# Rank 2 products of the gated layer's two projections, four at a time on the four row quarters of the array

## The chip, the cores and the metric

The kernel runs on one core of one Trainium2 chip. The metric is the device time of one execution in microseconds (us). The kernel before was timed three times.

## The reference

Four layers follow one another on a tensor x of 2 x 1024 tokens with 1024 channels, each as x = x + layernorm(layer(layernorm(x))). The change lies in the second of them, the gated layer. Cut to what matters:

```python
def _qlora_linear(x, wq, A, B):            # A: [2, in], B: [out, 2]
    w = jnp.tile(wq, (1, 4))               # wq: [out, in / 4]
    return x @ w.T + (x @ A.T @ B.T) * 0.5
gate = silu(_qlora_linear(x, w1q, a1, b1)) # w1q: [2752, 256]
up = _qlora_linear(x, w3q, a3, b3)
return _qlora_linear(gate * up, w2q, a2, b2)
```

Since the weight is tiled four times along the input, the kernel first adds the four parts of 256 input channels of x and multiplies the sum with the 256 columns of the quarter weight. The second term of each projection is a product of rank 2: two numbers a token (x @ A.T) times a row of B.

## The kernel before

The kernel is written in direct instructions with semaphores; each engine has one queue in a fixed order. The four layers are stages A, B, C and D. Stage B is the gated layer. It goes over 16 tiles of 128 tokens (t), and over 6 chunks (c) of 460 hidden columns (452 in the last). A pair (t, c) is a visit, numbered p = 6 t + c.

All large products are done in float32r. Each operand is split into a high part (rounded) and a low part (the rest), and three products are added: high x high, high x low, low x high. So a visit has, for the gate (v = 0) and for the up projection (v = 1), two halves of the 256 channels times three products, which are six matmuls of 128 rows, 128 tokens and 460 columns (lines 1126, 1127 and 1128 of `pe_up`).

To these comes one matmul for the rank 2 term (line 1133). Its stationary operand is `ux[:, par, v, :]`, 96 rows by 128 tokens; its moving operand is `bx[:, chunk]`, 96 rows by 460 columns. The rows of `bx` hold B of both projections three times, rounded in rows 0 to 31 and 64 to 95 and as the rest in rows 32 to 63 (`act_bhi` line 1211, `dve_blo` line 1339), and `ux` holds the two numbers a token rounded, rounded again, and the rest. With this the one matmul gives all three products. A visit of even number writes banks 0 (gate) and 1 (up) of PSUM, one of odd number banks 2 and 3. At its start a visit waits until the gate of visit p - 2 has read its banks (`gate_s(p - 1)`).

After a visit ScalarE takes the silu of the gate bank (`act_silu`, line 1259), VectorE multiplies it with the up bank (`dve_gate`, line 1356) and does two multiply and sum instructions for the rank 2 part of the third projection (`dve_acc`, line 1371), and GpSimd folds the product (`pool_gf`, lines 1469 and 1473).

Between the visits of tile t, TensorE also turns the folded result of tile t - 1 (`pe_gtr`, line 1146, after c = 0 and 2), multiplies it with the third weight (`pe_down`, lines 1159 to 1161, 18 matmuls of 512 columns after c = 3 and again after c = 4), and prepares tile t + 1:

- `pe_trans` (line 1088, after c = 1 and 2): transposes of x, which `act_xt` (line 1229) copies out.
- `pe_fold` (line 1099, after c = 3): x times A in float32, eight matmuls with 32 columns in the stationary operand, each four of them on the four column quarters of the array.
- `pe_low` (line 1107, after c = 4): two float32 matmuls with a constant matrix `sel`, which sum the four quarters, halve them and copy them to the rows where `ux` wants them, for v = 0 and v = 1. ScalarE reads the result with two instructions (`act_low`, lines 1250 and 1251), VectorE with one (`dve_low`, line 1350).

A float32 matmul is two records in the trace, a float32r matmul one.

The first tile of stage B (t = 0) stands between the last work of stage A. Its order is made by a planner (`plan`), which holds for each step an engine, a cost and the steps that it needs, and gives each engine a list. The planner orders the loads and stores of that time too: the load of `bx` (`sp_bx`), the stores of x (`stx`) and of its normalized form (`stn`), and the six loads of the third weight (`b_w2`). From t = 1 the order is the loops of `StageB.pe`, `act`, `dve` and `pool`. In tile 1 ScalarE also rounds the third weight (`act_w2hi`, line 1222) and VectorE and GpSimd form its rest (`w2lo`, line 1333).

Stage C is attention. Its matmuls with the values have 32 columns in the stationary operand and stand on the four column quarters as well (line 2001, float32). Its scores and maxima (lines 1986 and 1968) and its projections (lines 1944 to 1946) are float32r on the whole array.

Of the kernel before, what the change touches and what calls it, by code (L numbers as in the profile page):

```python
# [16 lines left out]
FH = 2752  # L17
# [236 lines left out]
class StageA:  # L254
# [78 lines left out]
    def plan(self):  # L333
# [102 lines left out]
        for c in range(3):  # L436
            add("act", .95, ("b_bhi", c), ("b_bx", 0), ("b_bhi", c - 1) if c else None)
            add("dve", 1.15, ("b_blo", c), ("b_bhi", c), ("b_blo", c - 1) if c else None)

        add("sp", 9.0, ("b_a2", 0), *(("conv", q, 2) for q in range(4)))  # L440
        add("sp", 3.5, ("b_bx", 0), ("down", 3, 3), ("center", 1, 8))
        add("sp", 1.0, ("b_a13", 0), layers, ("stn", 5))
# [5 lines left out]
        for t in range(2):  # L448
            for u in (2 * t, 2 * t + 1):
                add("pe", .5, ("b_tr", u), ("b_xn", t), ("b_xt", u - 1) if u % 2 else ("b_lowd", 0) if t else ("y", 12))  # L450
                add("act", .65, ("b_xt", u), ("b_tr", u), *((("b_fold", 0), ("b_xsum", 0)) if u == 2 else ()))
            add("pe", .9, ("b_fold", t), ("b_xt", 2 * t + 1), ("b_a13", 0))
            add("act", .3, ("b_usb", t), ("b_fold", t), ("b_low", 0) if t else None)
            add("pool", 2.1, ("b_xsum", t), ("b_xt", 2 * t + 1), ("b_xlo", 0) if t else None)
            add("act", .45, ("b_xhi", t), ("b_xsum", t))
            add("dve", .45, ("b_xlo", t), ("b_xhi", t))
            add("pe", .3, ("b_low", t), ("b_usb", t))
            add("act", .8, ("b_lowc", t), ("b_low", t))
# [524 lines left out]
class StageB:  # L983
# [3 lines left out]
    def __init__(self, k, first, x_src, xn_src, x_dst, xn_dst):  # L987
# [4 lines left out]
        with ExitStack() as ctx:  # L992
# [5 lines left out]
            self.w13l, self.w13h = sb("w13l", [128, 4 * FH], F32R), sb("w13h", [128, 4 * FH], F32R)  # L998
            self.bx = sb("bx", [96, FH], F32R)
            self.a13, self.sel = sb("a13", [128, 8, 32]), sb("sel", [128, 2, 96])  # L1000
            self.xnb = sb("xn", [128, 1024])
# [4 lines left out]
            self.usb = sb("usb", [128, 128])  # L1006
            self.ux, self.ur = sb("ux", [96, 2, 2, 128], F32R), sb("ur", [96, 2, 128], F32R)
            self.g = [sb(f"g{i}", [128, 460]) for i in range(3)]
            self.prod = [sb("pr0", [128, 460])]

            with nc.sbuf_tensor("b_bx_in", [96, FH], F32) as bx_in:
                self.bx_in = bx_in
# [30 lines left out]
    def sp_a13(self, e):  # L1043
        io = self.k.io
        e.dma_start(self.a13[:, :, :], io["a13T"].rearrange("(c p) n -> p c n", p=128)).then_inc(self.ldw.s, 16)
        e.dma_start(self.sel[:, :, :], io["sel"]).then_inc(self.ldw.s, 16)

# [55 lines left out]
    def pe_low(self, e, t):  # L1103
        e.wait_ge(*self.usb_s(t + 1))
        o = self.k.bank(5)
        for v in range(2):
            m = e.matmul(o[0:96, 128 * v:128 * v + 128], self.sel[:, v, :], self.usb[:, :], start=True, stop=True)
        m.then_inc(self.low_s.s, 1)

    def pe_up(self, e, t, c):  # L1110
# [3 lines left out]
        if t == 0:  # L1114
            e.wait_ge(*self.wlop_s(min(2 * c + 2, 6)))
            if c > 2:
                e.wait_ge(*self.wlod_s(2 * c - 4))
            if c < 2:
                e.wait_ge(*k.y_yn(self.first.tail.T + 14 + c))
        if p >= 2:  # L1120
            e.wait_ge(*self.gate_s(p - 1))
        wh, wl = self.chunk(self.w13h, c), self.chunk(self.w13l, c)
        for v in range(2):
            o = k.bank(2 * (p % 2) + v)[:, 0:n]
            for i in range(2):
                e.matmul(o, self.xsh[:, par, i, :], wh[:, v, i, :], start=i == 0, stop=False)  # L1126
                e.matmul(o, self.xsh[:, par, i, :], wl[:, v, i, :], start=False, stop=False)  # L1127
                e.matmul(o, self.xsl[:, par, i, :], wh[:, v, i, :], start=False, stop=False)  # L1128
# [73 lines left out]
    def act_bhi(self, e, i):  # L1202

        cols = slice(920 * i, min(920 * i + 920, FH))
        e.wait_ge(*self.ldb(1))
# [37 lines left out]
    def act_low(self, e, t):  # L1243
        e.wait_ge(*self.low_s(t + 1))
        if t > 0:
            e.wait_ge(*self.lowd_s(t))
        if t >= 2:
            e.wait_ge(*self.up_s(6 * (t - 1)))
# [87 lines left out]
    def dve_blo(self, e, i):  # L1336
        cols = slice(920 * i, min(920 * i + 920, FH))
        e.wait_ge(*self.bhi_s(i + 1))
        e.tensor_tensor(self.bx[32:64, cols], self.bx_in[32:64, cols], self.bx[32:64, cols].bitcast(F32), SUB
                        ).then_inc(self.blo_s.s, 1)  # L1340

# [5 lines left out]
    def dve_low(self, e, t):  # L1347
        e.wait_ge(*self.lowc_s(t + 1))
        o = self.k.bank(5)[:, 0:256].rearrange("p (v n) -> p v n", v=2)
        e.tensor_tensor(self.ux[64:96, t % 2, :, :], o[64:96], self.ur[64:96, :, :].bitcast(F32), SUB).then_inc(self.lowd_s.s, 1)  # L1350

# [1560 lines left out]
def lay_out(i):  # L2912
# [8 lines left out]
    cst[:, 256:384] = 1.0  # L2921
    cst[:, 384] = 1.0 / 128
    cst[:, 392:520] = np.where(np.arange(128)[None, :] > np.arange(128)[:, None], -1.0e38, 0.0)
    d["cst"] = cst
# [11 lines left out]
    d["w13"] = np.concatenate([w13[..., C0[c]:C0[c] + NS[c]].reshape(128, -1) for c in range(6)], 1)  # L2936
    bx = np.zeros((96, FH), f)
    for q in range(3):
        bx[32 * q:32 * q + 2] = g["L0_ffn_b1"][hid].T
        bx[32 * q + 2:32 * q + 4] = g["L0_ffn_b3"][hid].T  # L2940
    d["bx"] = bx
# [6 lines left out]
    d["w2x"] = np.concatenate([g["L0_ffn_w2q"].T, g["L0_ffn_b2"].T])  # L2948
    sel = np.zeros((128, 2, 96), f)
    for c in range(4):  # L2950
        for q in range(3):
            for r in range(2):
                sel[32 * c + r, 0, 32 * q + r] = 0.5
                sel[32 * c + 2 + r, 1, 32 * q + 2 + r] = 0.5
    d["sel"] = sel
# [26 lines left out]
```

## Time and profile before

| what | value |
|---|---|
| median of three runs | 2220.77 us (2220.75 to 2224.75) |
| the profiled execution, its own time | 2222.39 us |
| its span, first to last instruction | 2220.3 us |
| mean granted TensorE clock | 0.973 |
| busy: TensorE / its weight loads / VectorE / ScalarE / GpSimd | 93% / 67% / 64% / 43% / 45% |

A profile is of one execution. Busy time is the time in which an engine has at least one instruction under way. Matmuls are pipelined, so the record of one (about 0.37 us for 460 columns) overlaps the next; what a matmul costs in a dense stretch is the distance from its start to the next start. "PEld" is TensorE's weight load, which is a queue of its own beside the matmuls.

### The profile page before, as it was taken

Reading aid. Unit: us, or ns where it says so; the run is one execution under the profiler, and the core shown is the slowest. Engines: PE = TensorE matmul, PEld = TensorE weight load, DVE = VectorE, ACT = ScalarE, POOL = GpSimd, SP = SyncE. Lnnn points to the kernel's source line nnn. Section 1 sums busy time; section 2 is a strip of 40 time slices with the busy share of each in tenths; the row PEclk is TensorE's granted clock in tenths of the full one; section 3 lists DMA queues with packets and bytes.
Section 4 is the critical chain, followed back from the end, with each engine's and each line's share of the span. In section 5 each row is a group of like instructions: output and inputs, shape, how many; then the busy total and the mean of one; then the engine's idle time right before and its main releaser. Section 6 shows DMA issues by size and latency. Waiting matters only on the chain.

```text
span 2220.3 us, 30914 instructions
## 1 busy us (share of the span) xinstructions
PE 2057.5 (93%) x10568; PEld 1494.3 (67%) x10568; DVE 1411.5 (64%) x3276; ACT 955.2 (43%) x1990; POOL 997.1 (45%) x866
## 2 busy tenths in 40 slices
PE   5889987999999989989999999899998999999998
PEld 4645446788888879755556555555553688888887
DVE  6877766676776763387665677576768555544533
ACT  5755685232333323135554555455555332322311
POOL 1444586444444420018875586768873233120000
PEclk9999998999999999999999999999988999999999
DMA  6400275122211147422223723322223465544432
GB/s 186 172 2 29 101 248 213 39 76 77 74 67 68 68 173 272 121 53 55 68 71 100 212 66 78 78 77 72 52 68 121 137 225 174 167 161 138 134 117 92
DMA packets 148028, 249.78 MB, mean 112 GB/s; under 512 B 27150, under 2 KB 79246, under 8 KB 147648
## 3 DMA queue, kind: packets, MB, share of 16 engines
q1 hardware_dynamic: 136864, 227.89, 32.6%
q10 hardware_dynamic: 11008, 19.93, 2.9%
q8 instruction: 84, 1.38, 0.3%
q14 instruction: 72, 0.59, 0.1%
HBM read 140.01 MB, written 76.02 MB: 97 GB/s over the span
## 4 chain that ended last, share of the span: by engine, by line
PE 56%; POOL 15%; DVE 8%; issue 4%; DMA 3%; ACT 3%; SPq 1%; ACTq 1%; POOLq 0%; DVEq 0%
POOL c_S L2418 8%; PE PS L2609 4%; PE PS L2613 4%; PE PS L2610 4%; PE PS L1127 3%; PE PS L1126 3%; PE PS L1128 3%; PE PS L1986 3%; PE PS L1968 2%; PE PS L2001 2%; PE PS L1159 2%; PE PS L1161 2%; PE PS L1160 2%; DVE PS L2310 2%; PE PS L1944 2%
## 5 line engine op out<-in xcount | busy, mean ns | idle before, releaser
L2155 ACT ACTIVATE c_P<-PS 128x512 f32<-128x512 f32 (+3 forms) x768 | 357.3, 494 | 318.9 <-PE PS L1986 298.7
L1968 PE MATMUL PS<-c_K,c_Q 96*128 96x512 f32 (+3 forms) x768 | 276.2, 370 | 19.7 <-DVE cst L2310 13.9
L1986 PE MATMUL PS<-c_Q,c_K 97*128 97x512 f32 (+3 forms) x768 | 281.2, 380 | 7.0 <-DMA c_Q<-c_mT 4.3
L2418 POOL TENSOR_TENSOR c_S<-c_S,c_P 128x2048 f32<-128x2048 f32 (+3 forms) x94 | 272.7, 2901 | 8.6 <-ACT c_P L2155 0.2
L1986 PEld LDWEIGHTS PS<-c_Q,c_K 97*128 97x128 f32 x768 | 147.0, 194 | 174.4 <-ACT c_P L2155 97.2
L2306 DVE TENSOR_REDUCE cst<-PS 128x1 f32<-128x512 f32 x256 | 175.9, 687 | 91.4 <-PE PS L1968 91.0
L1968 PEld LDWEIGHTS PS<-c_K,c_Q 96*128 96x128 f32 x768 | 150.0, 196 | 75.0 <-DVE cst L2310 37.7
L2001 PE MATMUL PS<-c_P,c_V 128*32 128x512 f32 (+3 forms) x1536 | 168.2, 510 | 15.9 <-ACT c_P L2155 9.1
L2310 DVE CUSTOM_DVE_ANT_0 PS<-PS,maskw,cst 128x128 f32<-128x128 f32 (+3 forms) x256 | 142.8, 558 | 58.2 <-PE PS L1968 42.1
L213 POOL TENSOR_TENSOR maskw<-maskw,mhalf 128x1 f32<-128x1 f32 x64 | 38.6, 602 | 306.9 <-DVE maskw L171 297.9
L1259 ACT ACTIVATE b_g<-PS 128x460 f32<-128x460 f32 x96 | 53.0, 554 | 272.5 <-PE PS L1133 272.5
L2310 DVE CUSTOM_DVE_ANT_0 PS<-PS,maskw 128x128 f32<-128x128 f32 (+3 forms) x256 | 126.3, 503 | 63.0 <-PE PS L1968 61.2
L1371 DVE SCALAR_TENSOR_TENSOR b_pr<-b_g,b_a 128x460 f32<-128x460 f32 x192 | 159.9, 868 | 1.7
L2397 POOL TENSOR_SCALAR_AFFINE_SELECT c_P<-c_P 128x512 f32<-128x512 f32 x128 | 84.4, 660 | 159.2 <-ACT c_P L2155 159.2
L1469 POOL TENSOR_TENSOR b_gp<-b_g 128x230 f32<-128x230 f32 x96 | 84.5, 880 | 157.0 <-DVE b_g L1356 157.0
L1126 PE MATMUL PS<-b_w13h,b_xsh 128*128 128x460 f32 (+1 forms) x384 | 148.4, 386 | 5.4 <-ACT a_yl L230 3.3
L2609 PE MATMUL PS<-c_xth,d_xh 128*128 128x512 f32 x384 | 151.3, 394 | 0.0
L2610 PE MATMUL PS<-c_xtl,d_xh 128*128 128x512 f32 x384 | 150.1, 391 | 0.0
L1127 PE MATMUL PS<-b_w13l,b_xsh 128*128 128x460 f32 (+1 forms) x384 | 144.1, 375 | 0.0
L1128 PE MATMUL PS<-b_w13h,b_xsl 128*128 128x460 f32 (+1 forms) x384 | 143.2, 373 | 0.0
L1944 PE MATMUL PS<-c_xth,c_wh 128*128 128x512 f32 x304 | 125.5, 413 | 4.9 <-POOL c_wl L2239 2.3
L1356 DVE TENSOR_TENSOR b_g<-b_g,PS 128x460 f32<-128x460 f32 x96 | 60.4, 629 | 97.6 <-ACT b_g L1259 97.5
(301 smaller groups left out, 4887.8 us busy)
## 6 DMA issues: line engine op xcount, KB each, us to landing
a_xin<-in_x SPq DMA_DIRECT2D x32, 512.0 KB, 4.6
d_x<-scr SPq DMA_DIRECT2D x32, 512.0 KB, 4.8
c_Q<-c_qh SPq DMA_DIRECT2D x240, 64.0 KB, 2.0
scr<-a_xin SPq DMA_DIRECT2D x16, 512.0 KB, 6.7
b_xn<-scr SPq DMA_DIRECT2D x16, 512.0 KB, 5.7
b_x<-scr SPq DMA_DIRECT2D x16, 512.0 KB, 4.8
scr<-b_x SPq DMA_DIRECT2D x16, 512.0 KB, 2.6
scr<-b_y SPq DMA_DIRECT2D x16, 512.0 KB, 3.0
```

Source lines behind the costliest of these rows:

```text
L1126: e.matmul(o, self.xsh[:, par, i, :], wh[:, v, i, :], start=i == 0, stop=False)
L1127: e.matmul(o, self.xsh[:, par, i, :], wl[:, v, i, :], start=False, stop=False)
L1128: e.matmul(o, self.xsl[:, par, i, :], wh[:, v, i, :], start=False, stop=False)
L1968: e.matmul(bank[:, 0:hi - lo], self.Q4[0:96, 4 * (o % 3) + g, 128 * t:128 * t + 128], self.K4[0:96, HEADS[o % 8], lo:hi], start=True, stop ...
L1986: e.matmul(self.k.bank(i % 3)[:, 0:hi - lo], self.K4[0:97, HEADS[o % 8], 128 * kt:128 * kt + 128], self.Q4[0:97, 4 * (o % 3) + g, lo:hi], ...
L2001: m = e.matmul(k.bank(5)[32 * g:32 * g + 32, lo - 512 * half:512], self.V[:, kt, o // 8, HEADS[o % 8], :], P[:, g, 0:hi - lo], start=kt == ...
L2155: e.activation(self.P[:, R % 3, g, 0:hi - lo], self.k.bank(i % 3)[:, 0:hi - lo], ACT.Exp, scale=SCALE).then_inc(self.exp_s.s, 1)
L2306: e.tensor_reduce(m, r, AX, ALU.max).then_inc(self.mx_s.s, 1)
L2310: e.tensor_tensor_reduce(out=r, in0=r, in1=self.maskw[:, 512 - n:512], scale=1.0, scalar=m if lo > 0 else -3.0e38, op0=ADD, op1=ALU.max, a ...
L2418: e.tensor_tensor(S[:, :, 512 - n:512], S[:, :, 512 - n:512], P[:, :, 0:n], ADD).then_inc(self.psum_s.s, 1)
L2609: e.matmul(o, h, wh[:, c, cols], start=c == 0, stop=False)
L2610: e.matmul(o, h, wl[:, c, cols], start=False, stop=False)
```

## The change

The three products of a rank 2 term need only six rows of the array, so they fit in one quarter of 32 rows. The kernel after puts the gate and the up projection of an even chunk in row quarters 0 and 1, and those of the odd chunk behind it in quarters 2 and 3. Four matmuls with 32 rows each (`tile_position=(32 * s, 0)`) write banks 0, 1, 2 and 3. They are issued one after another at the end of the even visit, as the last addends of banks 0 and 1 and the first addends of banks 2 and 3; the odd visit has no rank 2 matmul. Before the four, TensorE waits for `gate_s(p)`, the gate of the odd visit before, since banks 2 and 3 are written now; the odd visit has no wait of its own any more. In tile 0 the wait for stage A's last users of banks 2 and 3 moves from visit 1 to the four in visit 0.

`ux`, `ur`, `bx` and `sel` change their form: `ux` is 128 rows by 128 tokens a tile (before: 96 rows by 256), `bx` is 128 rows by 3 x 460 columns (before: 96 by 2752), `sel` one matrix of 128 by 128 (before: two of 128 by 96), so `pe_low` is one float32 matmul, `act_low` one copy of 128 by 128, and `dve_low` and `dve_blo` one scalar_tensor_tensor over all 128 rows with a mask as scalar. Three unused tensors keep the later addresses about where they were. The planner's costs and conditions follow.

```diff
-                ("b_up", c - 1) if c else None, ("b_gate", c - 2) if c > 1 else ("y", 13 + c))
+                ("b_up", c - 1) if c else None, ("b_gate", c - 1 - c % 2) if c > 1 else ("y", 14))
...
     def pe_low(self, e, t):
         e.wait_ge(*self.usb_s(t + 1))
         o = self.k.bank(5)
-        for v in range(2):
-            m = e.matmul(o[0:96, 128 * v:128 * v + 128], self.sel[:, v, :], self.usb[:, :], start=True, stop=True)
-        m.then_inc(self.low_s.s, 1)
+        e.matmul(o[:, 0:128], self.sel[:, :], self.usb[:, :], start=True, stop=True).then_inc(self.low_s.s, 1)
...
-            if c < 2:
-                e.wait_ge(*k.y_yn(self.first.tail.T + 14 + c))
-        if p >= 2:
+            if c == 0:
+                e.wait_ge(*k.y_yn(self.first.tail.T + 14))
+        if p >= 2 and c % 2 == 0:
             e.wait_ge(*self.gate_s(p - 1))
         wh, wl = self.chunk(self.w13h, c), self.chunk(self.w13l, c)
+        late = c % 2
         for v in range(2):
-            o = k.bank(2 * (p % 2) + v)[:, 0:n]
+            o = k.bank(2 * late + v)[:, 0:n]
             for i in range(2):
...
-            if c == 0 and v == 0:
-                e.wait_ge(*self.lowd_s(t + 1))
-            if t == 0 and c % 2 == 0 and v == 0:
-                e.wait_ge(*self.blo_s(c // 2 + 1))
-            m = e.matmul(o, self.ux[:, par, v, :], self.bx[:, C0[c]:C0[c] + n], start=False, stop=True)
-        m.then_inc(self.up_s.s, 1)
...
+        if late:
+            m.then_inc(self.up_s.s, 1)
+        else:
+            self.pe_rank(e, t, c // 2)
+
+    def pe_rank(self, e, t, j):
+
+        k, p, par = self.k, 6 * t + 2 * j, t % 2
+        if j == 0:
+            e.wait_ge(*self.lowd_s(t + 1))
+        if t == 0:
+            e.wait_ge(*self.blo_s(j + 1))
+            if j == 0:
+                e.wait_ge(*k.y_yn(self.first.tail.T + 15))
+        if p > 0:
+            e.wait_ge(*self.gate_s(p))
+        for s in range(4):
+            n, rows = NS[2 * j + s // 2], slice(32 * s, 32 * s + 32)
+            m = e.matmul(k.bank(s)[:, 0:n], self.ux[rows, par, :], self.bx[rows, 460 * j:460 * j + n], start=s > 1, stop=s < 2,
+                         skip_group_check=True, tile_position=(32 * s, 0))
+            if s == 1:
+                m.then_inc(self.up_s.s, 1)
...
-        o = self.k.bank(5)[:, 0:256].rearrange("p (v n) -> p v n", v=2)
-        e.copy(self.ux[0:64, t % 2, :, :], o[0:64])
-        e.copy(self.ur[64:96, :, :], o[64:96]).then_inc(self.lowc_s.s, 1)
+        e.copy(self.ur[:, :], self.k.bank(5)[:, 0:128]).then_inc(self.lowc_s.s, 1)
...
-        e.tensor_tensor(self.ux[64:96, t % 2, :, :], o[64:96], self.ur[64:96, :, :].bitcast(F32), SUB).then_inc(self.lowd_s.s, 1)
+        if t >= 2:
+            e.wait_ge(*self.up_s(6 * (t - 1)))
+        e.scalar_tensor_tensor(out=self.ux[:, t % 2, :], in0=self.k.bank(5)[:, 0:128], scalar=self.k.cst[:, 385:386],
+                               in1=self.ur[:, :].bitcast(F32), op0=MUL, op1=SUB).then_inc(self.lowd_s.s, 1)
```

## Rows read from the trace of the kernel before

**Rows 1.** Windows by stage: length, busy (instructions) by engine, clock, DMA share, GB/s

```profile
380.00:420.00 40.00, 32.77 (x150) 28.11 (x151) 26.65 (x47) 12.57 (x22) 22.34 (x21) 0.83 0.09 27
750.00:780.00 30.00, 30.00 (x164) 26.13 (x163) 21.68 (x49) 8.78 (x16) 13.09 (x17) 1.00 0.25 85
```

**Rows 2.** Waits, 450 to 800 us: total us, times, longest

```profile
ACT b_g L1259 <- PE PS L1133: 212.8, 73, 5.4
```

**Rows 3.** The critical chain in order of time: start, us, what

```profile
329.06 0.86 PE PS L617 x2
...
393.87 0.76 PE PS L1159
...
489.03 0.44 PE PS L1107 x4
...
773.96 0.44 PE PS L1107 x4
...
793.99 0.23 PE PS L1160
...
807.76 0.56 ACT b_g L1259
```

**Rows 4.** TensorE, timeline 602 to 613 us: start, duration, line

```profile
602.84 0.60 PE L1107 MATMUL PS<-b_usb,b_sel 128*96 128x128 f32 x4
603.20 0.48 PE L1159 MATMUL PS<-b_w2h,b_gfh 115*128 115x512 f32 x1
603.52 0.40 PE L1160 MATMUL PS<-b_w2l,b_gfh 115*128 115x512 f32 x1
...
610.27 0.37 PE L1126 MATMUL PS<-b_w13h,b_xsh 128*128 128x460 f32 x1
...
612.99 0.38 PE L1133 MATMUL PS<-b_bx,b_ux 96*128 96x460 f32 x1
```

**Rows 5.** TensorE, timeline around the fold on four column quarters

```profile
623.30 0.37 PE L1133 MATMUL PS<-b_bx,b_ux 96*128 96x460 f32 x1
623.60 0.64 PE L1099 MATMUL PS<-b_xT,b_a 128*32 128x128 f32 x16
624.17 0.50 PE L1159 MATMUL PS<-b_w2h,b_gfh 115*128 115x512 f32 x1
624.51 0.39 PE L1160 MATMUL PS<-b_w2l,b_gfh 115*128 115x512 f32 x1
```

**Rows 6.** TensorE, timeline around a group of stage C on column quarters

```profile
1301.43 0.28 PE L1968 MATMUL PS<-c_K,c_Q 96*128 96x256 f32 x1
1301.65 1.06 PE L2001 MATMUL PS<-c_P,c_V 128*32 128x512 f32 x8
1302.64 0.44 PE L1986 MATMUL PS<-c_Q,c_K 97*128 97x384 f32 x1
1302.92 0.34 PE L1968 MATMUL PS<-c_K,c_Q 96*128 96x384 f32 x1
```

**Rows 7.** The weight loads of that group, timeline

```profile
1301.64 0.16 PEld L2001 LDWEIGHTS PS<-c_P,c_V 128*32 128x32 f32 x8 [0.20 <-issue]
1302.64 0.19 PEld L1986 LDWEIGHTS PS<-c_Q,c_K 97*128 97x128 f32 x1 [0.84 <-ACT c_P L2155]
```

**Rows 8.** Weight loads by line: ns min/median/max, first and last start

```profile
L1133 PEld LDWEIGHTS PS<-b_bx,b_ux x192: 187/188/334, 340.8 to 807.2; 96*128 96x128 f32 x192
...
L2001 PEld LDWEIGHTS PS<-c_P,c_V x1536: 106/109/155, 981.4 to 1736.4; 128*32 128x32 f32 x192
```

**Rows 9.** VectorE, timeline: the gate of a tile's last visit

```profile
611.05 0.62 DVE L1356 TENSOR_TENSOR b_g<-b_g,PS 128x452 f32<-128x452 f32 x1 [1.75 <-ACT b_g L1259]
```

**Rows 10.** Tiles 0 and 1: TensorE, ScalarE and GpSimd rows

```profile
348.00 0.72 PE L1126 MATMUL PS<-b_w13h,b_xsh 128*128 128x460 f32 x1 [3.29 <-ACT a_yl L230]
...
378.43 1.99 ACT L1222 CAST b_w2h<-b_w 115x1024 fp32r<-115x1024 f32 x2 [6.87 <-DMA b_w<-in_w2x]
...
L1333 POOL TENSOR_TENSOR b_w2l<-b_w,b_w2h x3: 2356/3322/3354, 379.6 to 390.5; 115x1024 fp32r<-115x1024 f32 x3
```

More of the change, by code:

```diff
@@ L436, in plan @@
         for c in range(3):
-            add("act", .95, ("b_bhi", c), ("b_bx", 0), ("b_bhi", c - 1) if c else None)
-            add("dve", 1.15, ("b_blo", c), ("b_bhi", c), ("b_blo", c - 1) if c else None)
+            add("act", .5, ("b_bhi", c), ("b_bx", 0), ("b_bhi", c - 1) if c else None)
+            add("dve", .65, ("b_blo", c), ("b_bhi", c), ("b_blo", c - 1) if c else None)
         add("sp", 9.0, ("b_a2", 0), *(("conv", q, 2) for q in range(4)))
-        add("sp", 3.5, ("b_bx", 0), ("down", 3, 3), ("center", 1, 8))
+        add("sp", 2.5, ("b_bx", 0), ("down", 3, 3), ("center", 1, 8))
         add("sp", 1.0, ("b_a13", 0), layers, ("stn", 5))
@@ L457, in plan @@
             add("pe", .3, ("b_low", t), ("b_usb", t))
-            add("act", .8, ("b_lowc", t), ("b_low", t))
+            add("act", .3, ("b_lowc", t), ("b_low", t))
             add("dve", .45, ("b_lowd", t), ("b_lowc", t))
@@ L998, in __init__ @@
             self.w13l, self.w13h = sb("w13l", [128, 4 * FH], F32R), sb("w13h", [128, 4 * FH], F32R)
-            self.bx = sb("bx", [96, FH], F32R)
-            self.a13, self.sel = sb("a13", [128, 8, 32]), sb("sel", [128, 2, 96])
+            self.bx = sb("bx", [128, 3 * 460], F32R)
+            sb("gap0", [128, 1368])
+            self.a13, self.sel = sb("a13", [128, 8, 32]), sb("sel", [128, 128])
+            sb("gap1", [128, 64])
             self.xnb = sb("xn", [128, 1024])
@@ L1006, in __init__ @@
             self.usb = sb("usb", [128, 128])
-            self.ux, self.ur = sb("ux", [96, 2, 2, 128], F32R), sb("ur", [96, 2, 128], F32R)
+            self.ux, self.ur = sb("ux", [128, 2, 128], F32R), sb("ur", [128, 128], F32R)
+            sb("gap2", [128, 384])
             self.g = [sb(f"g{i}", [128, 460]) for i in range(3)]
             self.prod = [sb("pr0", [128, 460])]
-            with nc.sbuf_tensor("b_bx_in", [96, FH], F32) as bx_in:
+            with nc.sbuf_tensor("b_bx_in", [128, 3 * 460], F32) as bx_in:
                 self.bx_in = bx_in
@@ L1045, in sp_a13 @@
         e.dma_start(self.a13[:, :, :], io["a13T"].rearrange("(c p) n -> p c n", p=128)).then_inc(self.ldw.s, 16)
-        e.dma_start(self.sel[:, :, :], io["sel"]).then_inc(self.ldw.s, 16)
+        e.dma_start(self.sel[:, :], io["sel"]).then_inc(self.ldw.s, 16)
     def sp_a2(self, e):
@@ L1125, in pe_up @@
             for i in range(2):
-                e.matmul(o, self.xsh[:, par, i, :], wh[:, v, i, :], start=i == 0, stop=False)
-                e.matmul(o, self.xsh[:, par, i, :], wl[:, v, i, :], start=False, stop=False)
-                e.matmul(o, self.xsl[:, par, i, :], wh[:, v, i, :], start=False, stop=False)
-            if c == 0 and v == 0:
-                e.wait_ge(*self.lowd_s(t + 1))
-            if t == 0 and c % 2 == 0 and v == 0:
-                e.wait_ge(*self.blo_s(c // 2 + 1))
@@ L1133, in pe_up @@
-            m = e.matmul(o, self.ux[:, par, v, :], self.bx[:, C0[c]:C0[c] + n], start=False, stop=True)
-        m.then_inc(self.up_s.s, 1)
+                e.matmul(o, self.xsh[:, par, i, :], wh[:, v, i, :], start=i == 0 and not late, stop=False, skip_group_check=True)
+                e.matmul(o, self.xsh[:, par, i, :], wl[:, v, i, :], start=False, stop=False, skip_group_check=True)
+                m = e.matmul(o, self.xsl[:, par, i, :], wh[:, v, i, :], start=False, stop=i == 1 and bool(late),
+                             skip_group_check=True)
@@ L1202, in act_bhi @@
     def act_bhi(self, e, i):
-        cols = slice(920 * i, min(920 * i + 920, FH))
+        cols = slice(460 * i, 460 * i + 460)
         e.wait_ge(*self.ldb(1))
@@ L1336, in dve_blo @@
     def dve_blo(self, e, i):
-        cols = slice(920 * i, min(920 * i + 920, FH))
+        cols = slice(460 * i, 460 * i + 460)
         e.wait_ge(*self.bhi_s(i + 1))
-        e.tensor_tensor(self.bx[32:64, cols], self.bx_in[32:64, cols], self.bx[32:64, cols].bitcast(F32), SUB
-                        ).then_inc(self.blo_s.s, 1)
+        e.scalar_tensor_tensor(out=self.bx[:, cols], in0=self.bx_in[:, cols], scalar=self.k.cst[:, 386:387],
+                               in1=self.bx[:, cols].bitcast(F32), op0=MUL, op1=SUB).then_inc(self.blo_s.s, 1)
     def dve_xlo(self, e, t):
@@ L2922, in lay_out @@
     cst[:, 384] = 1.0 / 128
+    for s in range(4):
+        cst[32 * s + 4:32 * s + 6, 385] = 1.0
+        cst[32 * s + 2:32 * s + 4, 386] = 1.0
     cst[:, 392:520] = np.where(np.arange(128)[None, :] > np.arange(128)[:, None], -1.0e38, 0.0)
@@ L2936, in lay_out @@
     d["w13"] = np.concatenate([w13[..., C0[c]:C0[c] + NS[c]].reshape(128, -1) for c in range(6)], 1)
[L2937 to L2940, printed above, removed]
+    bx = np.zeros((128, 3 * 460), f)
+    for c in range(6):
+        rows, cols = 64 * (c % 2), 460 * (c // 2)
+        for q in range(3):
+            for v, n in enumerate(("L0_ffn_b1", "L0_ffn_b3")):
+                bx[rows + 32 * v + 2 * q:rows + 32 * v + 2 * q + 2, cols:cols + NS[c]] = g[n][hid[C0[c]:C0[c] + NS[c]]].T
     d["bx"] = bx
@@ L2948, in lay_out @@
     d["w2x"] = np.concatenate([g["L0_ffn_w2q"].T, g["L0_ffn_b2"].T])
-    sel = np.zeros((128, 2, 96), f)
+    sel = np.zeros((128, 128), f)
     for c in range(4):
[L2951 to L2954, printed above, removed]
+        for s in range(4):
+            for q in range(3):
+                for r in range(2):
+                    sel[32 * c + 2 * (s % 2) + r, 32 * s + 2 * q + r] = -0.5 if q else 0.5
     d["sel"] = sel
```

3 lines of the change are left out of this document (removed).

## The prediction

> **What bounds the kernel now.** I read the windows by stage first. From about 394 to 808 us TensorE is busy all the time at the full clock of 2.4 GHz, while VectorE is busy 22 of 30 us, and DMA a quarter of the time; in 380 to 420 us TensorE has gaps and a granted clock of 0.83 [rows 1]. The waits say the same: ScalarE waits 213 of 350 us for the rank 2 matmul that ends a visit [rows 2]. The chain of waits is TensorE alone, and gives the period: `pe_low` of one tile starts at 489.03, that of the tenth after it at 773.96, so a tile takes 28.49 us [rows 3]. Whatever a tile loses on TensorE in this stretch shortens the kernel, until another engine is late.
>
> Two ends have to be drawn. At the start, tile 0 and most of tile 1 are not TensorE's: ScalarE waits 6.9 us for the third weight's load until 378.43, GpSimd's last part of its rest starts at 390.5 and takes 3.3 us [rows 10], and the first `pe_down` of stage B starts at 393.87 [rows 3]. What TensorE saves before 393.87 is waited away. The stage's last silu is at 807.76 [rows 3], and what follows (the last tile's way out, stage C's first tiles) starts from it, so I take the saving as passed on in full. Between lie, of the changed pieces: the four of visit 4 of tile 1, three groups of four in each of tiles 2 to 15, so 43 groups, and `pe_low` in tiles 1 to 14, 14 times.
>
> **What is removed: four rank 2 matmuls in a row of visits.** From visit 0's first start at 610.27 to its 14th at 612.99 are 13 steps, 0.209 us each [rows 4]. The record's 0.37 us is not the cost, since records overlap. Four cost 0.837 us.
>
> **What is added: one group on row quarters.** No group on row quarters stands in this trace. The nearest are groups on column quarters, in two places. In stage C, four float32 matmuls of 512 columns [rows 6]. Before it, the 256 column matmul steps 0.22 us where by columns (0.23 us for 512 in the chain, L1160 at 793.99) it should be 0.12 [rows 3]: 0.10 to enter. The group takes 0.99; one float32 matmul of 512 columns alone takes 0.86 in the chain [rows 3], so the four do run side by side, with 0.13 over one. Behind it the 384 column matmul steps 0.28 instead of 0.17: 0.11 to leave. Sum over the stream: 0.34. The fold gives the same: 0.30 instead of 0.21 on entering, 0.57 for two float32 matmuls of 128 columns in series (2 x 0.86 / 4 = 0.43), 0.34 instead of 0.23 on leaving, again 0.34 [rows 5]. What the entry and exit are is seen in the weight loads: in a dense stretch a load starts a matmul ahead, but the group's first load starts only at 1301.64, with the matmul, after a pause of 0.20, and the load behind it at 1302.64, with its matmul too [rows 7]. So neither is hidden.
>
> The changed group streams 460 columns once: 0.209. To this the 0.34, and its first load is longer: 188 ns for 128 columns against 109 for 32 [rows 8], so 0.08. The group costs 0.63, and saves 0.837 - 0.63 = 0.21 us; times 43 is 9.0 us. The eight loads of the group in stage C lie within 0.16 us, 0.05 more than one, so 7 ns apart [rows 7]; I take it that loads on row quarters overlap so too.
>
> Bounds. Below: nothing for entering and leaving, 0.209 + 3 x 0.007 = 0.23, saves 0.61 a group, 26 us. Above, in two steps. Loads that follow one another: (188 - 109) / 96 columns is 0.82 ns a column [rows 8], 0.105 for 128, three times 0.32, so the group is 0.95 and loses 0.11, 5 us in all. And matmuls that don't run side by side at all: 0.837 + 0.34 + 0.08 = 1.26, loses 0.42, 18 us. I take the value between since it is the one that both places of the trace give, with the same 0.34.
>
> The Trainium skill, page "TensorEngine Tiling (Array Packing)", Key Properties, says that a change of the tiling mode, not of the tile alone, drains TensorE. The trace agrees for column quarters, by the 0.10 on entering and on leaving. By this rule the sum stays at 9.0 us; it speaks against the small groups of this change, of which each pays both ways.
>
> **`pe_low`: two float32 matmuls to one.** Four records start at 602.84, the next line's first at 603.20 and second at 603.52 [rows 4]; less one step of 0.23 for the latter the four cost 0.45. Half of it goes: 0.22 x 14 = 3.1 us. The load is of 128 columns instead of 96; half of 0.45 for two passes leaves 0.11 a load, just enough for 0.105. Bounds 1.5 and 3.1 us.
>
> **Other edits.** `act_low` (one instruction instead of two), `dve_low` and the casts of `bx` lie beside a TensorE that is the later one, and don't set the end; ScalarE waits over half of the time [rows 2]. If that cover were gone they would gain less than 1 us a tile, not lose. The matmuls' count and columns in the visits stay. `dve_low` now holds the wait for `up_s` of the tile before, which is long passed.
>
> **Waits that move.** The group waits for the gate of the odd visit before it. Behind it in the queue stands all of TensorE. The tightest is visit 0: its twelve other matmuls end 12 x 0.209 = 2.5 us after 610.27, at 612.78, and the gate of the last visit ends at 611.05 + 0.62 = 611.67 [rows 4, 9]. Slack 1.1 us. After the other odd visits stand transposes or a `pe_down`, so more. In tile 0 the group waits for stage A's y, for which visit 1 waited 3.29 us until 348.00 [rows 10]; so visit 0 ends and its silu starts some 5.6 us later than before. Cover: ScalarE's 6.9 us for the third weight [rows 10]. That load's place in SP's queue comes from the planner, behind stores of stage A that a late VectorE or GpSimd moves; with fewer and shorter steps, but later ones, I take zero, and 3 us on either side for the range.
>
> **Sum.** Span 2220.3 - 9.0 - 3.1 = 2208.2. The profiled execution took 2222.39, 1.6 above the median of 2220.77, so its time would be 2210.3 and the median 2208.7 us.
>
> **Rivals.**
> 1. Loads hidden, no entry or exit: the group's four loads start under the full matmul before, as loads in a dense stretch do, and the next full load starts under the group. For it: with whole-array matmuls the trace shows just this. Against it: at both places with quarters it doesn't [rows 5, 7]. 26 + 3.1 us less: 2191.5 us. The page "TensorE: Matmul & The Clock Gate" of the Trainium skill, Part 3, The mechanism, has the loads pulled ahead where row groups don't conflict, and starts some 4 ns apart; its measured speedup of four row quarters (3.07) would make 0.27 of the 0.837, so 24 us; no run here shows it yet.
> 2. Half of it: only entering or leaving is paid. 0.43 a group, saves 0.41, 17.5 us and 3.1: 2200 us.
> 3. The other side: the row quarters' loads or matmuls stand in line. The change decides against itself when a group costs over 0.837 + 3.1 / 43 = 0.91 us. With loads in line 0.95: 5 - 3.1 = 2 us more, 2222.7. With matmuls in line: 18 - 3.1, 2235.7. For it: no row shows row quarters at work; against it, the column quarters' loads lie 7 ns apart.
> 4. A new wait: the gate of visit 5 comes later than the group. Each 0.1 us beyond the slack of 1.1 costs 15 x 0.1 = 1.5 us; from 0.9 us beyond it the gain of 12 is gone. For it: VectorE is busy 72% [rows 1] and the tile gets 4% shorter. Against: the slack is as long as the gate and the silu together.
> 5. The gain is real but lost on the way to the end, at the load of the third weight or at stage C's first loads: 2217 to 2223.
>
> **Chances.** Forecast (2204 to 2213 by itself) 0.42; rival 1 0.20; rival 2 0.12; rival 3 0.12, a third of it with matmuls in line; rival 4 0.06; rival 5 0.08. A measurement of this kernel tells 0.2%, 4.4 us, from no change. Faster by more than that: 0.42 + 0.20 + 0.12 and a little of 4: 0.75. Within: two thirds of rival 3, most of 5, some of 4: 0.14. Slower: 0.11. The range goes from rival 1 to loads in line: 2190 to 2222; only matmuls in line and the worst of 4 and 5 are outside, and some of the faster side.
>
> **What the profile after would show.** Right: a tile's period, `pe_low` to `pe_low`, of 28.49 - 3 x 0.21 - 0.22 = 27.64 us; the first of the four some 0.31 behind the last full matmul's start; the four starts within 0.03 us, their loads too; the matmul behind the group 0.1 late. A period of 26.4 is rival 1, 28.6 rival 3 with loads in line. Rival 4 would show as idle TensorE before the group in visit 0, released by VectorE's gate. The first `pe_down` should stay within 3 us of 393.87. Wrong would be the prediction above all by the group's cost: each 0.1 us of it is 4.3 us of time.

## The result, and the profile after

The kernel after takes 2203.61 us (median of six runs, 2199.94 to 2205.72), the kernel before, run beside it, 2221.57 us. The ratio is 0.9914 with a 95% interval of 0.9900 to 0.9927, so about 18 to 19 us are gained. The forecast was 2208.7 us, that is 12.1 gained.

The profiled execution after took 2203.54 us, its span is 2201.4 us, 18.9 less than before. The windows by stage (length, busy time of TensorE, its loads, VectorE, ScalarE, GpSimd, granted clock, DMA share, GB/s) answer to [rows 1]:

```profile
380.00:420.00 40.00, 36.48 (x190) 29.58 (x189) 27.10 (x53) 10.32 (x19) 22.94 (x23) 0.87 0.07 27
750.00:780.00 30.00, 30.00 (x147) 24.89 (x147) 22.39 (x54) 7.09 (x12) 13.18 (x18) 1.00 0.14 53
```

TensorE still has no gap in the stage and the full clock, but its loads are busy 24.9 of 30 us instead of 26.1. The chain of waits from tile 0 on, and its end in stage B (start, us, what), answers to [rows 3]:

```profile
355.10 17.69 DMA b_w<-in_w2x
...
388.27 0.77 PE PS L1178
...
788.86 0.56 ACT b_g L1274
```

The same row of the kernel before:

```profile
361.48 16.93 DMA b_w<-in_w2x
```

The third weight's last load is issued at 355.10 (361.48 before) and takes 17.7 us. The first down product is at 388.27 instead of 393.87, the last silu at 788.86 instead of 807.76. From the one to the other are 400.6 us instead of 413.9, 13.3 less; behind the last silu stand 2201.4 - 788.9 = 1412.5 us, and 2220.3 - 807.8 = 1412.5 before, so in these two executions what the stage gains reaches the end in full. The other 5.6 us are gained before the first down product. The loads of x's tiles in stage A, with SP's stores between them left out (timeline of SP), show how they split:

```profile
252.09 0.38 SPq L141 DMA_DIRECT2D a_xin<-in_x  x1
...
346.96 0.33 SPq L141 DMA_DIRECT2D a_xin<-in_x  x1
```

```profile
250.73 0.38 SPq L141 DMA_DIRECT2D a_xin<-in_x  x1
...
342.02 0.33 SPq L141 DMA_DIRECT2D a_xin<-in_x  x1
```

The first fence is the kernel before, the second the kernel after. The load of tile 4 is 1.4 us earlier already, far from any change; that of tile 15 4.9 us earlier. From the load of tile 4 to the first down product are 141.8 us before and 137.5 after: 4.2 us are gained there, and 1.4 come from how this execution began: in the fourteen executions below that load is issued between 250.6 and 255.2.

The group itself, TensorE's timeline behind the last matmuls of visit 0 and of visit 2:

```profile
599.92 0.36 PE L1130 MATMUL PS<-b_w13h,b_xsl 128*128 128x460 f32 x1
600.22 0.48 PE L1150 MATMUL PS<-b_bx,b_ux 32*128 32x460 f32 x4
600.63 0.69 PE L1165 MATMUL PS<-cst,b_gf 128*115 128x128 f32 x4
...
606.41 0.37 PE L1130 MATMUL PS<-b_w13h,b_xsl 128*128 128x460 f32 x1
606.71 0.48 PE L1150 MATMUL PS<-b_bx,b_ux 32*128 32x460 f32 x4
607.12 0.47 PE L1165 MATMUL PS<-cst,b_gf 128*115 128x128 f32 x2
607.43 0.60 PE L1091 MATMUL PS<-cst,b_xn 128*128 128x128 f32 x4
```

The kernel before, behind the rank 2 matmul of visit 2:

```profile
619.71 0.37 PE L1133 MATMUL PS<-b_bx,b_ux 96*128 96x460 f32 x1
619.92 0.38 PE L1146 MATMUL PS<-cst,b_gf 128*115 128x128 f32 x2
620.14 0.60 PE L1088 MATMUL PS<-cst,b_xn 128*128 128x128 f32 x4
```

The first of the four starts 0.30 us behind the matmul before, not 0.21: 0.09 to enter. All four lie in 0.48 us, where one record alone has 0.47 (below), so they start within 0.01 us. The next line starts 0.41 later, and its two records take 0.31 (607.12 to 607.43) where the same two took 0.22 in the kernel before (619.92 to 620.14). That is 0.09 + 0.41 + 0.09 = 0.59 us a group. The loads of the two groups (timeline of the weight loads), and by line over the whole kernel (ns min/median/max):

```profile
600.22 0.19 PEld L1150 LDWEIGHTS PS<-b_bx,b_ux 32*128 32x128 f32 x4 [0.31 <-issue]
600.63 0.49 PEld L1165 LDWEIGHTS PS<-cst,b_gf 128*115 128x115 f32 x4 [0.22 <-issue]
...
606.70 0.19 PEld L1150 LDWEIGHTS PS<-b_bx,b_ux 32*128 32x128 f32 x4 [0.32 <-issue]
```

```profile
L1150 PEld LDWEIGHTS PS<-b_bx,b_ux x192: 181/181/285, 344.7 to 781.6; 32*128 32x128 f32 x192
L1150 PE MATMUL PS<-b_bx,b_ux x192: 446/472/751, 344.7 to 781.6; 32*128 32x460 f32 x160, 32*128 32x452 f32 x32
```

Four loads fit in 0.19 us, where one takes 0.181: they run at the same time, and start with the matmuls after 0.31 of pause. The low matmul after, with ten periods between these two lines:

```profile
480.52 0.49 PE L1109 MATMUL PS<-b_usb,b_sel 128*128 128x128 f32 x2
...
756.02 0.49 PE L1109 MATMUL PS<-b_usb,b_sel 128*128 128x128 f32 x2
```

(756.02 - 480.52) / 10 = 27.55 us a tile, 0.94 less than the 28.49 of [rows 3].

### The profile page after: what moved, and what is told of

The parts are those of the page before. It is cut to its first block, busy times and chain, and to the rows that moved or that the text cites. A ratio compares the mean times of both kernels' runs of the same rounds, so it can differ in the third digit from the quotient of the medians.

```text
span 2201.4 us, 30864 instructions
## 1 busy us (share of the span) xinstructions
PE 2039.6 (93%) x10536; PEld 1460.6 (66%) x10536; DVE 1408.6 (64%) x3276; ACT 947.2 (43%) x1974; POOL 1002.1 (46%) x866
## 4 chain that ended last, share of the span: by engine, by line
PE 56%; POOL 14%; DVE 9%; issue 4%; ACT 2%; DMA 2%; SPq 1%; ACTq 1%; POOLq 0%; DVEq 0%
POOL c_S L2435 8%; PE PS L2626 5%; PE PS L2627 4%; PE PS L2630 4%; PE PS L1128 3%; PE PS L1129 3%; PE PS L1130 3%; PE PS L2003 3%; PE PS L2018 3%; PE PS L1985 3%; PE PS L1178 2%; PE PS L1179 2%; DVE PS L2327 2%; PE PS L1180 2%; PE PS L1961 2%
## 5 line engine op out<-in xcount | busy, mean ns | idle before, releaser
L1985 PE MATMUL PS<-c_K,c_Q 96*128 96x512 f32 (+3 forms) x768 | 276.6, 370 | 20.8 <-DVE cst L2327 13.3
L1962 PE MATMUL PS<-c_xtl,c_wh 128*128 128x512 f32 x304 | 121.4, 399 | 0.0
```

Source lines behind the costliest of these rows:

```text
L1985: e.matmul(bank[:, 0:hi - lo], self.Q4[0:96, 4 * (o % 3) + g, 128 * t:128 * t + 128], self.K4[0:96, HEADS[o % 8], lo:hi], start=True, stop ...
```

## The experiments

Each run is compared with the kernel before on the same chip. The runs were made in several series, in which the kernel before had medians of 2221.57 (beside after) and 2222.80 to 2223.85, so times of different series are compared by their ratios. For the stage I read three numbers from each profile: the period of a tile (ten `pe_low` apart, as above), the distance from the load of x's tile 4 to the first down product, and the time behind the last silu.

| kernel | median us | ratio to before (95%) | period | tile 4 to first down | behind last silu |
|---|---|---|---|---|---|
| before | 2221.57 | 1 | 28.49 | 141.8 | 1412.5 |
| after | 2203.61 | 0.9914 (0.9900 to 0.9927) | 27.55 | 137.5 | 1412.5 |
| whole_array | 2214.95 | 0.9963 (0.9946 to 0.9980) | 28.23 | 137.5 | 1417.3 |
| same_quarter | 2232.78 | 1.0040 (1.0022 to 1.0058) | 29.38 | 137.0 | 1406.6 |
| two_of_four | 2204.85 | 0.9911 (0.9877 to 0.9946) | 27.56 | 137.7 | 1414.1 |
| two_pairs | 2227.73 | 1.0011 (0.9994 to 1.0027) | 29.13 | 137.4 | 1410.1 |
| before_newcosts | 2223.60 | 1.0007 (0.9991 to 1.0022) | 28.49 | 141.6 | 1416.1 |
| after_oldcosts | 2207.33 | 0.9940 (0.9917 to 0.9962) | 27.55 | 141.5 | 1416.0 |
| low_twice | 2210.44 | 0.9953 (0.9937 to 0.9970) | 27.78 | 137.4 | 1417.8 |
| before_ldx11 | 2224.21 | 1.0005 (0.9990 to 1.0020) | 28.49 | 141.6 | 1415.7 |
| after_ldx11_late | 2208.98 | 0.9936 (0.9911 to 0.9961) | 27.55 | 137.5 | 1415.0 |
| fold_next | 2206.63 | 0.9923 (0.9900 to 0.9945) | 27.40 | 137.4 | 1420.3 |
| oldplan_newsp | 2208.88 | 0.9937 (0.9916 to 0.9958) | 27.55 | 138.5 | 1415.2 |
| newplan_oldsp | 2210.04 | 0.9941 (0.9923 to 0.9958) | 27.55 | 139.6 | 1413.0 |

The time behind the last silu is that of stages C and D, with the same instructions in all, and lies between 1406.6 and 1420.3 from one execution to another. Part of this goes with TensorE's clock: in same_quarter, the shortest, the mean granted clock over the span is 0.974, in fold_next, the longest, 0.966. The three kernels with before's instructions have 1414.8 there on average, the five with after's (after, after_oldcosts, after_ldx11_late, oldplan_newsp, newplan_oldsp) 1414.3, so the gain of the stage is not lost behind it. From the first down product to the last silu the three take 413.6 to 414.0 us and the five 398.2 to 401.1, so the gain in the stage is known to 1 or 2 us, and of whole times even less: after_ldx11_late has the period and the distance of after, and its ratio gives 14 us where after's gives 19. So I judge single steps by the period, which repeats to 0.01 us.

**whole_array: the group without quarters.**

```diff
-            m = e.matmul(k.bank(s)[:, 0:n], self.ux[rows, par, :], self.bx[rows, ...], ..., tile_position=(32 * s, 0))
+            m = e.matmul(k.bank(s)[:, 0:n], self.ux[:, par, :], self.bx[:, ...], ...)
```

> The kernel after, but the four rank 2 matmuls of a group stand on the whole array: 128 rows, no tile position (each then adds the products of all four quarters, so the output is another one). Place, waits, order of work and the single low matmul stay. Theory (the gain in the stage is the group's streams side by side, less entering and leaving): the group costs 4 x 0.209 = 0.84 us instead of the 0.60 read from the trace after, so 43 x 0.24 = 10 us more than after's 2203.6: 2214; the period of a tile goes from 27.55 to 28.27. Rival (the gain comes from where the group stands and from the planner's new order, not from the quarters): 2203 to 2206, period near 27.6.

Measured: period 28.23, so 0.68 for three groups, 0.226 a group; the theory said 0.24. TensorE's timeline around a group:

```profile
611.98 0.98 PE L1150 MATMUL PS<-b_bx,b_ux 128*128 128x460 f32 x4
612.80 0.38 PE L1165 MATMUL PS<-cst,b_gf 128*115 128x128 f32 x2
613.02 0.60 PE L1091 MATMUL PS<-cst,b_xn 128*128 128x128 f32 x4
```

The four take 0.82 to the next start, and that one steps 0.22 and not 0.31. So 9.7 of the stage's 13.2 us hang on the quarters. Against before 0.266 us a tile are left, of which low_twice (below) gives 0.227 to the low matmul; the group's place at the end of the even visit brings at most the other 0.04.

**same_quarter: four on one quarter.**

```diff
-            m = e.matmul(k.bank(s)[:, 0:n], self.ux[rows, par, :], self.bx[rows, ...], ..., tile_position=(32 * s, 0))
+            m = e.matmul(k.bank(s)[:, 0:n], self.ux[0:32, par, :], self.bx[0:32, ...], ..., tile_position=(0, 0))
```

> The kernel after, but all four matmuls of a group stand on row quarter 0 (rows 0 to 31 for all, so the output is another one). Same mode, same number of columns and loads, but no two can run side by side. Theory (entering and leaving are paid by any group with 32 rows, and on one quarter the streams follow one another): 0.84 + 0.39 = 1.23 us a group, 0.63 more than after, 43 x 0.63 = 27 us: 2231; period 29.4. Rival (a group on quarter 0 alone is no change of mode, since it starts at row 0 like the whole array): 0.84 a group, 2214; period 28.3.

Measured: period 29.38, 0.61 a group more than after; 2232.78 us, slower than before. Timeline of the matmuls and of the weight loads at one group:

```profile
618.42 0.37 PE L1130 MATMUL PS<-b_w13h,b_xsl 128*128 128x460 f32 x1
618.72 1.08 PE L1150 MATMUL PS<-b_bx,b_ux 32*128 32x460 f32 x4
619.74 0.47 PE L1165 MATMUL PS<-cst,b_gf 128*115 128x128 f32 x2
620.05 0.60 PE L1091 MATMUL PS<-cst,b_xn 128*128 128x128 f32 x4
```

```profile
618.72 0.71 PEld L1150 LDWEIGHTS PS<-b_bx,b_ux 32*128 32x128 f32 x4 [0.32 <-issue]
```

Entering (0.30) and what is late behind (0.31) are those of after; the middle is 1.02 instead of 0.41, three steps of 0.20 more. The loads take 0.71 and not 0.19. So the price of entering and leaving is there on quarter 0 as well, and where the streams don't run side by side the change loses: it is rival 3's case.

**two_of_four: half of the group left out.** `for s in range(4)` becomes `for s in range(2)`, and the odd visit's first matmul starts its banks.

> The kernel after, but only the two matmuls of the even visit are issued (quarters 0 and 1); the rank 2 products of the odd chunks are left out. Theory (all four run side by side with loads side by side too): nothing changes, 2203.6, a group still 0.60, period 27.55. Rival (part of the group's 0.41 between its first start and the next is loads or starts in line, 0.02 to 0.1 us for each): 43 x 2 x 0.02 to 0.1 = 2 to 9 us faster, 2195 to 2202.

Measured: period 27.56, the same to 0.01 us. The third and fourth matmul cost nothing at all.

**two_pairs: twice as many groups.**

```diff
-        if late:
-            m.then_inc(self.up_s.s, 1)
-        else:
-            self.pe_rank(e, t, c // 2)
+        self.pe_rank(e, t, c // 2, late)
...
-        for s in range(4):
+        for s in range(2 * late, 2 * late + 2):
```

> The kernel after, but each visit has its own two rank 2 matmuls at its end: the even one on quarters 0 and 1, the odd one on quarters 2 and 3, with the waits of the kernel before. Same matmuls in all, twice as many groups. Theory (0.60 a group, whatever is in it): 43 more groups of 0.60, 26 us more than after, 2229, so slower than before (2221.6); period 29.35. Rival (the cost goes with the number of matmuls, so that a pair costs 0.30 to 0.42, as two steps of 0.209 do): 2203 to 2214.

Measured: period 29.13, so 0.53 for an added group, 0.07 less than expected, and the gain is gone: no difference from before that the interval shows. The added groups don't cost the same. Here are the one of visit 3, with the fold on column quarters behind it, and the one of visit 5, with a full matmul behind it:

```profile
597.62 0.37 PE L1130 MATMUL PS<-b_w13h,b_xsl 128*128 128x460 f32 x1
597.92 0.47 PE L1143 MATMUL PS<-b_bx,b_ux 32*128 32x460 f32 x2
598.33 0.64 PE L1102 MATMUL PS<-b_xT,b_a 128*32 128x128 f32 x16
598.90 0.50 PE L1170 MATMUL PS<-b_w2h,b_gfh 115*128 115x512 f32 x1
...
612.86 0.36 PE L1130 MATMUL PS<-b_w13h,b_xsl 128*128 128x452 f32 x1
613.16 0.48 PE L1143 MATMUL PS<-b_bx,b_ux 32*128 32x452 f32 x2
613.56 0.47 PE L1128 MATMUL PS<-b_w13h,b_xsh 128*128 128x460 f32 x1
613.88 0.37 PE L1129 MATMUL PS<-b_w13l,b_xsh 128*128 128x460 f32 x1
```

From 612.86 to 613.88 are 1.02 us, where two steps of 0.21 would be: the group costs 0.60. The fold enters by 0.30 and takes 0.57 in after too, so the pair before it costs only the 0.41 from 597.92 to 598.33. The third, before visit 1's transposes, makes the rest of 3 x 0.526, 0.57 by this sum. A pair with the whole array on both sides costs more than two steps there, 0.42; one with column quarters behind it costs as much.

**low_twice.** One more `e.matmul(o[:, 128:256], self.sel[:, :], self.usb[:, :], ...)` before the low matmul.

> The kernel after, with the low matmul issued twice, the first time into columns that nobody reads. Theory (a float32 matmul of 128 columns and its 128 column load cost 0.22 us on TensorE's path, 14 or 15 times in the stage): 3.1 us slower than after, 2206.7; period 27.77. Rival (it stood in the shadow of the group's leaving or of the load for the next matmul): under 1 us, 2204; period 27.6.

Measured: period 27.78, 0.23 a tile, as said. The whole time doesn't show it so well: the ratio is 0.9953 where after's, of another series, is 0.9914, which is 8.7 us, and 14 tiles give 3.2. In the profiled execution 5.3 us of the difference lie behind the last silu, where no instruction differs.

**before_newcosts and after_oldcosts.** The four costs of the planner, changed in the one and changed back in the other:

```diff
-            add("act", .95, ("b_bhi", c), ...
-            add("dve", 1.15, ("b_blo", c), ...
-        add("sp", 3.5, ("b_bx", 0), ...
-            add("act", .8, ("b_lowc", t), ...
+            add("act", .5, ("b_bhi", c), ...
+            add("dve", .65, ("b_blo", c), ...
+        add("sp", 2.5, ("b_bx", 0), ...
+            add("act", .3, ("b_lowc", t), ...
```

> The kernel before, with the four changed costs of the planner (rounding of bx 0.5 and 0.65, its load 2.5, the copy of low 0.3) and nothing else: conditions and instructions are those of before. In tile 0 the order on ScalarE, VectorE, GpSimd and SP shifts somewhat. Theory (the 5.6 us by which the first down product came earlier, 388.27 against 393.87, come from the order of the loads and stores that the planner gives, above all from the last load of x standing ahead of, not behind, the load of tile 2's normalized x): in this kernel too the last load of the third weight lands some us off 378.4, and the time moves with it; its SP order puts these two loads as before does or as after does, and the time follows: 2221.6 with the order of before. Rival (smaller loads of bx and shorter instructions bring it): no order matters, 2221.6 whatever the order.

> The kernel after, with the four costs of the planner as in the kernel before. The instructions are those of after, only the order in tile 0 differs. Theory (order of loads and stores): the stage from the first down product on stays at 400.6 us, and the first down product comes at another time than 388.27, between 384 and 396, so 2199 to 2211. Rival (5.6 us come from the smaller load and the shorter instructions): first down product at 388 again and 2203.6.

Measured: 141.6 us from tile 4 to the first down product in the one, 141.5 in the other. With the old costs 4.0 of the 4.2 us fall away though every instruction is that of after, so after's order is needed for them; shorter instructions and the smaller `bx` alone don't bring them. Whether after's order would bring them with before's instructions was not run. The new costs alone don't bring them either, although with them too the last load of x stands ahead of the load of tile 2's normalized x: that detail is not the cause.

The traces tell where the 4 us are. In all fourteen the first down product stands 15.4 to 15.5 us behind the start of ScalarE's rounding of the third weight's last part, that is, behind that load's landing. With after's order (after and seven others, after_ldx11_late among them) the load is issued 104.2 to 104.6 us behind the load of tile 4 and the rounding starts at 121.6 to 122.2. In before, before_newcosts, before_ldx11 and after_oldcosts it is issued at 109.4, 107.2, 110.5 and 108.3, and the rounding starts at 126.3, 126.2, 126.1 and 126.1: between these four it does not follow the issue of the last load. What it does follow there is open.

**before_ldx11 and after_ldx11_late.** One entry of SP's list moved, after the plan is made:

```diff
+        sp = self.order["sp"]
+        sp.remove(("ldx", 11))
+        sp.insert(sp.index(("ldx", 10)) + 1, ("ldx", 11))
```

(the second with `("b_a13", 0)` in place of `("ldx", 10)`).

> The kernel before, with one entry of SP's list in tile 0 moved: the load of x's tile 11 stands right behind that of tile 10 (as in the kernel after) instead of behind the load of the a13 matrix. Between the load of x's tile 4 and the first down product lie 141.8 us in the kernel before, 141.6 with the new costs, 141.5 in the kernel after with the old costs, and 137.1 to 137.6 in five kernels with after's order. Theory (this one place makes the 4.2 us: the load is issued 10 us later where it stands behind the normalized x's store and load): here the distance is 137.6 and the time 2217.5. Rival (it is the order on ScalarE, VectorE and GpSimd): the distance stays at 141.5 to 141.8, and the time at 2221.6.

> The kernel after, with the load of x's tile 11 moved back behind the load of the a13 matrix in SP's list, nothing else. Theory (as for before_ldx11): the distance from the load of x's tile 4 to the first down product goes from 137.5 to 141.7, and the time from 2203.6 to 2207.8. Rival (order on the other engines): 137.5 and 2203.6.

Measured: 141.6 and 137.5. My theory of the one load fell; its place alone does nothing.

**oldplan_newsp and newplan_oldsp.** SP's list written out, the compute engines' order of the other plan:

```diff
+        self.order["sp"] = [...]
```

> The kernel after with the planner's old costs (as after_oldcosts), so the order in tile 0 on TensorE, ScalarE, VectorE and GpSimd of that one, but with SP's list of loads and stores of the kernel after, written out. From the load of x's tile 4 to the first down product lie 141.5 us in after_oldcosts and 137.5 in after. Theory (SP's order as a whole makes the 4.1 us, though the place of one load alone did not): 137.5 here, time near 2203.6. Rival (the compute engines' order makes it): 141.5, time near 2207.5.

> The mirror image: the kernel after with its own order on the four compute engines, but with SP's list as the old costs give it. Theory (SP's order): 141.5 and 2207.5. Rival (the compute engines' order): 137.5 and 2203.6. If both this and oldplan_newsp lie near 141.5, it takes both.

Measured: 138.5 and 139.6. SP's order of after on the old compute order brings 3.0 of the 4.0 us, the compute order of after on the old SP list 1.9. So the full 4.0 take both, SP's list more. The whole times don't tell these two from each other or from after_oldcosts.

**fold_next: a try for more.**

```diff
-                    if c == 3:
+                    if c == 4:
                         self.pe_fold(e, t + 1)
-                    if c == 4:
-                        self.pe_low(e, t + 1)
                 if c in (3, 4):
                     self.pe_down(e, t - 1, c - 3)
+                if t + 1 < NT and c == 4:
+                    self.pe_low(e, t + 1)
```

(ScalarE's `act_usb` moves to c = 4, its `act_low` and VectorE's `dve_low` ahead of the silu and the gate of c = 5.)

> A try for a faster kernel: in tiles 1 to 14 the fold for the next tile, which stands on column quarters, is moved from behind visit 3 to right behind the group on row quarters of visit 4, and the low matmul from there to behind the second down product; ScalarE's and VectorE's readers move with them. Theory (a change between two kinds of quarters is one drain and one short load, so row quarters to column quarters saves one return to the whole array: 0.09 to leave, 0.11 of load, less 0.03): 0.17 us a tile, period 27.38, 2.5 us faster than after: 2201. Rival (the cost belongs to each group, whatever stands beside it): period 27.55, 2203.6. If the fold's readers come late, VectorE's gate of visit 5 is behind the low and the period is longer.

Measured: period 27.40, 0.15 less than after; the fold starts 0.41 behind the group, as any next line does, and takes 0.57 to the next start, as it does behind visit 3 in after. So its own entering, 0.09 of the 0.15, is gone; the other 0.06, where the low matmul has moved too, are not taken apart:

```profile
480.78 0.48 PE L1150 MATMUL PS<-b_bx,b_ux 32*128 32x460 f32 x4
481.19 0.65 PE L1102 MATMUL PS<-b_xT,b_a 128*32 128x128 f32 x16
481.76 0.50 PE L1178 MATMUL PS<-b_w2h,b_gfh 115*128 115x512 f32 x1
```

In the whole time this is not seen: 0.9923 against after's 0.9914, in intervals that overlap, with 1420.3 us behind the last silu in the profiled execution. The step is shown in the stage, a faster kernel is not.

## Why the prediction was right, point by point

- **What bounds the stage.** Right. TensorE has no gap from the first down product on, and 13.3 us less between it and the last silu arrive at the end as 13.3. That the two profiles have the same 1412.5 us behind it is chance, but on average nothing is lost there (above).
- **The group's cost.** Forecast 0.63 us, of which entering and leaving 0.34, stream 0.21, a longer load 0.08. From the timeline 0.59, from whole_array 0.837 - 0.226 = 0.61. The terms taken from column quarters hold for row quarters: 0.09 to enter and 0.09 on what follows, where 0.10 and 0.11 were read in stage C, and between them 0.20 over one stream of 0.21, where 0.13 and a longer load of 0.08 were said. That four loads overlap, taken from rows of stage C, is shown by two_of_four. 43 groups give 9.7 us where 9.0 were said.
- **`pe_low`.** 0.22 forecast, 0.227 measured by doubling; 3.2 us of 3.1.
- **The stage in sum.** 13.3 us where 12.1 were said. 14 periods of 0.943 are 13.2; the 13.3 of one pair of profiles is itself good to 1 or 2 us only. Of the 0.943 the quarters make 0.677 and the low matmul 0.227, and 0.04 are left: not resolved.
- **The step that was mis-sized.** "With fewer and shorter steps, but later ones, I take zero, and 3 us on either side": the load of the third weight came 4.2 us earlier, and after_oldcosts shows that this needs the planner's new order. The profiled execution was forecast at 2210.3 and took 2203.54: of these 6.8 us 4.2 are this, 1.2 the stage, and 1.4 the execution's own start, which is luck. The sign could not be read from the trace of before, and zero was taken for it; 3 us on either side were too few.
- **What the time alone can say.** 2203.61 lies just below the 2204 to 2213 that the forecast gave itself, and not far above rival 2's 2200. The period tells them apart: 27.55 us, with 27.64 forecast and 28.49 - 3 x 0.41 - 0.22 = 27.04 for rival 2.
- **Waits that move.** Right for the stage, wrong in tile 0. The gate of a tile's last visit starts at 598.41 and takes 0.63, the group of visit 0 starts at 600.22 (timeline of VectorE, and above of TensorE), so 1.2 us of slack where 1.1 were said:

```profile
598.41 0.63 DVE L1373 TENSOR_TENSOR b_g<-b_g,PS 128x452 f32<-128x452 f32 x1 [1.33 <-ACT b_g L1274]
```

  In tile 0 the group of visit 0 was said to wait for stage A's y, as visit 1 had. It did not: the group starts at 344.72, 0.31 behind its visit's last matmul. ScalarE had made a y at 337.27 to 338.38 and makes the next at 346.67 only, so the one that the group needs was there 6 us before it. Visit 0's silu starts at 345.52 and not at 342.96, 2.6 us later where 5.6 were said. The stall that is long came in tile 1, before the group of visit 2, while the third weight is loaded and rounded; the kernel before stood still nearly as long there, before its transposes (after first, before second, then ScalarE after, with the end of that load):

```profile
377.97 0.76 PE L1150 MATMUL PS<-b_bx,b_ux 32*128 32x460 f32 x4 [6.45 <-DVE b_g L1373]
383.29 1.12 PE L1088 MATMUL PS<-cst,b_xn 128*128 128x128 f32 x4 [5.86 <-ACT b_xT L1229]
372.82 1.99 ACT L1241 CAST b_w2h<-b_w 115x1024 fp32r<-115x1024 f32 x2 [6.12 <-DMA b_w<-in_w2x]
```

  It costs nothing: the first down product starts 15.4 us behind that load's end in both.
- **The rivals.** Rival 1 (everything hidden) would have shown a period of 26.4 and loads ahead of the group; the loads start with it. Rival 2 is out with 0.09 paid on both sides. Rival 3's dearer half, matmuls in line, was made by same_quarter and costs what it was priced at (0.61 more a group, of 0.63); loads in line without it were not run. Rival 4 did not come; a new wait of ScalarE for VectorE's `dve_acc` (11 times 1.9 us) has TensorE's work before it and costs nothing. Rival 5 did not come; at the load of the third weight time was gained, not lost.
- **The rule of the pages.** That a change of the mode drains TensorE, as the page "TensorEngine Tiling (Array Packing)" of the Trainium skill has it under Key Properties, agrees with the groups shown here: 0.30 instead of 0.21 into each. That loads are pulled ahead where row groups don't conflict ("TensorE: Matmul & The Clock Gate", Part 3, The mechanism) agrees inside the group, four loads in 0.19 us, and not at its edge, where the pause before them is 0.31.

## What to carry to other kernels

Matmuls of few rows on row quarters are worth it by the group: here one paid 0.4 us to enter, load and leave and a single stream of 0.2, so four for one win 0.23, and a pair loses unless column quarters follow. Put as many as there are free banks into one group, and try groups of either kind of quarters side by side: the stage here was 0.15 us a tile faster by it, the whole time not visibly. And when a change touches a planner's costs, run it with the old order too, before the whole gain is put down to the change.

## What was not expected of the hardware

- A group of two and one of four on row quarters cost the same to 0.01 us a tile (27.56 and 27.55), weight loads included: four loads of 128 columns lie in 0.19 us on four quarters, and in 0.71 on one.
- A group that stands on quarter 0 alone, and so starts at row 0 like the whole array, pays the same entering and leaving (steps of 0.30 and 0.31) as one over four quarters.
- From row quarters right to column quarters costs less than by way of the whole array: 0.15 us a tile in fold_next, and in two_pairs 0.41 for the pair before the fold against 0.60 for the pair before a full matmul.
- The same stages C and D took between 1406.6 and 1420.3 us behind stage B in fourteen profiled executions, with the same instructions. From 500 to 950 us behind the last silu the granted clock is 0.98 in the shortest and 0.95 in the longest.
